# Attention and dense layers: four products with v in one go, maxima and closes in steps, five banks in one ring

## What is computed

```python
xn = _layernorm(x)
x = x + _L0_attn_ref(xn, ...) + _L0_ffn_ref(xn, ...)
xn = _layernorm(x)
x = x + _L1_attn_ref(xn, ...) + _L1_ffn_ref(xn, ...)
```

## Time and profile before

| | |
|---|---|
| median of three runs | 2231.34 us (2224.88 to 2234.45) |
| the profiled execution, its own time | 2234.62 us |
| its span, first to last instruction | 2232.8 us |
| mean granted TensorE clock | 0.924 |
| TensorE, matmuls | 1884.2 us busy (84%) |
| VectorE | 1211.5 us (54%) |
| ScalarE | 1096.7 us (49%) |
| GpSimd | 824.9 us (37%) |
| TensorE's part of the chain that ended last | 63% |

### The profile page before, as it was taken

One profiled execution on the slowest core, in us unless ns is written; L12 is line 12 of the kernel. 1 busy time (PEld: TensorE's weight loads), 2 busy tenths in 40 slices (PEclk: granted clock), 3 DMA queues, 4 the chain that ended last, 5 costly groups with the idle time before them and its releaser, 6 DMA issues.

```text
span 2232.8 us, 32221 instructions
## 1 busy us (share of the span) xinstructions
PE 1884.2 (84%) x10777; PEld 910.8 (41%) x10777; DVE 1211.5 (54%) x3653; ACT 1096.7 (49%) x2178; POOL 824.9 (37%) x935
## 2 busy tenths in 40 slices
PE   3573899999799999988778888888888898888877
PEld 2340455555245444422333444444344443444334
DVE  4554455555544444467555646657566565664653
ACT  0232455565455555545554545446455464554544
POOL 2215221111011111155575545465454554552520
PEclk8566899999999999989998999999999999999999
DMA  7244343333634244445234534344434344352240
GB/s 144 70 143 125 72 83 78 79 74 86 194 59 65 45 60 60 67 98 72 37 55 58 72 49 60 51 64 58 58 52 69 47 57 70 44 72 39 36 52 20
DMA packets 145972, 155.91 MB, mean 70 GB/s; under 512 B 26008, under 2 KB 132784, under 8 KB 145808
## 3 DMA queue, kind: packets, MB, share of 16 engines
q1 hardware_dynamic: 123872, 114.75, 33.1%
q0 software_dynamic: 10048, 14.44, 3.8%
q10 hardware_dynamic: 11888, 24.64, 3.2%
HBM read 55.95 MB, written 33.72 MB: 40 GB/s over the span
## 4 chain that ended last, share of the span: by engine, by line
PE 63%; DVE 10%; ACT 7%; POOL 7%; issue 6%; DMA 4%; SPq 3%; ACTq 0%; DVEq 0%; POOLq 0%
PE p_PV L937 11%; PE p_S L897 9%; PE p_S L918 8%; PE p_Mb L990 3%; PE p_S L1013 3%; DVE p_S L1125 3%; SPq L1884 3%; ACT t_R L1478 3%; PE p_Ma L870 2%; PE p_S L922 2%; PE p_S L870 2%; DMA t_NM<-hTd 2%; PE p_Mb L870 1%; PE p_Ma L806 1%; PE p_Mb L806 1%
## 5 line engine op out<-in xcount | busy, mean ns | idle before, releaser
L1478 ACT ACTIVATE t_R<-p_S 128x512 f32<-128x512 f32 (+1 forms) x1216 | 676.8, 575 | 489.3 <-PE p_S L922 269.8
L1125 DVE CUSTOM_DVE_ANT_0 p_S<-p_S,t_R 128x128 f32<-128x128 f32 (+3 forms) x1024 | 478.5, 515 | 295.0 <-PE p_S L897 294.7
L918 PE MATMUL p_S<-t_R 99*128 99x512 bf16 (+3 forms) x1536 | 485.5, 341 | 65.7 <-ACT t_R L1478 64.5
L897 PE MATMUL p_S<-t_R 96*128 96x512 bf16 (+3 forms) x1536 | 465.9, 344 | 83.2 <-DVE t_mx L1125 38.5
L1131 DVE TENSOR_REDUCE t_mx<-p_S 128x1 f32<-128x512 f32 x512 | 345.2, 684 | 303.4 <-PE p_S L897 277.7
L937 PE MATMUL p_PV<-t_R 128*17 128x512 f32 (+3 forms) x3072 | 338.6, 514 | 4.2 <-ACT t_R L1478 2.8
L897 PEld LDWEIGHTS p_S<-t_R 96*128 96x128 bf16 x1536 | 138.1, 99 | 414.5 <-issue 149.8
L918 PEld LDWEIGHTS p_S<-t_R 99*128 99x128 bf16 x1536 | 154.2, 100 | 218.5 <-ACT t_R L1478 112.9
L1681 POOL CAST t_spl<-t_rr 128x512 bf16<-128x512 f32 x80 | 49.0, 613 | 436.9 <-DVE t_rr L1088 436.9
L922 PE MATMUL p_S<-t_R,t_B1T 128*128 128x128 bf16 x1024 | 204.7, 225 | 0.0
L1125 DVE DVE_READ_ACCUMULATOR2_ANT t_mx<- 128x1 f32 x1024 | 142.4, 139 | 0.0
(11 more groups left out here) (299 smaller groups left out, 2505.7 us busy)
## 6 DMA issues: line engine op xcount, KB each, us to landing
t_R<-t_spl SPq DMA_DIRECT2D x480, 128.0 KB
t_R<-in_w ACTq DMA_DIRECT2D x32, 512.0 KB, 10.7
t_R<-ks SPq DMA_DIRECT2D x96, 128.0 KB
ks<-t_spl SPq DMA_DIRECT2D x16, 384.0 KB, 7.1
hTd<-t_NM SPq DMA_DIRECT2D x39, 128.0 KB
ysd<-t_NM SPq DMA_DIRECT2D x39, 128.0 KB
t_NM<-hTd SPq DMA_DIRECT2D x39, 128.0 KB, 2.3
ysd<-t_NM POOLq DMA_DIRECT2D x39, 128.0 KB, 3.1
```

Source lines behind the costliest of these rows:

```text
L897: t = self.nc.tensor.matmul(bank[:, z, :], qa[0:96, h, qb * 128:(qb + 1) * 128], ka[0:96, h, 0:n], start=True, stop=True)
L918: t = self.nc.tensor.matmul(bank[:, z, :], ka[0:99, h, kb * 128:(kb + 1) * 128], qa[0:99, h, n0:512], start=True, stop=not u.causal)
L1125: x = nc.vector.tensor_tensor_reduce(out=sc, in0=sc, in1=m.maskq[:, 512 - n:512], scale=1.0, scalar=NEG, op0=ALU.add, op1=ALU.max, accum_o ...
L1478: nc.scalar.activation(m.P1X[kb][j0 // per] if u.causal else m.P[p % 2][:, j0:j0 + per, :], m.s2_bank(k)[:, 0:per * n].rearrange("p (j n) ...
```

## The change

**Products.** In layer 1 `expp` keeps all four key blocks of a group, and `finish` issues their four products in one step, after the second scores of the next group. In layer 0 each key block stays by itself.

**Closes.** `finish` no longer adds steps. It sets a generator `closing`, of which each scores step without a `finish` takes one step: unload, in layer 1 an empty one, TensorE's `turn_o`, then `settle`.

**Maxima.** `maxp` becomes `top` (product and maximum) and a generator `shift`, of which each `top` but the first of a group takes one step during the next group: `turn_m` (TensorE), `shift_first` (ScalarE, the first of the four small instructions) and `shift_rest` (VectorE, the second), `shift_second` (ScalarE, the third), `shift_third` (VectorE, the fourth), `shift_rows` (SP).

**Projections.** A projection takes three steps: `project` on TensorE; `first` on ScalarE and `rest` on VectorE; `spread` on GpSimd and SP. v takes two, `project` and `keep`. The convolution does the same. The lane's empty tail grows from 9 (or 6) to 26 steps, the head start of the first and last convolution from 5 to 18.

**Banks.** `MB` gets the two banks of the maxima as fourth and fifth. Up to round 14 three go round, and `top` uses the other two in turn. From round 15 on five go round and the causal `top` takes from the same ring. The turned maxima take a bank of the ring in both layers.

**Experts.** The two halves of `up` and of `down` are one step each; the shares per round are rescaled (40 to 28, 24 to 14, 35 to 21).

```diff
@@ rounds
+        if i == 15:
+            e.ring = 5
         if 1 <= i < 6:
-            lanes.append(take(first, 40))
+            lanes.append(take(first, 28))
@@ Memory
-        self.MB = [ps("Ma"), ps("Mb"), self.S1[2]]
+        self.MB = [ps("Ma"), ps("Mb"), self.S1[2], self.S1[0], self.S1[1]]
@@ Engine.bank
         self.banks += 1
-        return self.banks % 3
+        return self.banks % self.ring
+
+    def top_bank(self, u):
+
+        if u.causal:
+            return self.bank()
+        self.tops += 1
+        return 3 + self.tops % 2
@@ Engine.pre
                 if u.b in (0, NB - 1):
-                    yield from steps(5)
+                    yield from steps(18)
                 for cc in range(2):
                     self.turn_c(u.b, cc, self.bank())
                     yield
-            self.convolve(u, self.bank())
-            yield
-            yield from steps(6)
+            i = self.bank()
+            self.convolve(u, i)
+            yield
+            self.first(u, 0, i)
+            self.rest(u, 0, i)
+            yield
+            self.spread(u, 0)
+            self.spread(u, 1)
+            yield
+            yield from steps(26)
             return
@@ Engine.project_unit
-        for z in range(3):
-            self.project0(u, z, self.bank())
-            yield
+
+        for z in range(2):
+            i = self.bank()
+            self.project(u, z, i)
+            yield
+            self.first(u, z, i)
+            self.rest(u, z, i)
+            yield
+            self.spread(u, z)
+            yield
+        i = self.bank()
+        self.project(u, 2, i)
+        yield
+        self.keep(u, i)
+        yield
@@ Engine.maxp
     def maxp(self, u):
-        return steps(s1_uses(u))
+
+        for g in range(2):
+            for x, p in enumerate(packs_of(u)):
+                self.top(u, g, p, self.top_bank(u))
+                if x:
+                    next(self.chain, None)
+                yield
+            self.chain = self.shift(u, g)
+        if u.n == 47:
+            yield from self.chain
+    def shift(self, u, g):
+
+        i = self.bank()
+        self.turn_m(u, g, i)
+        yield
+        self.shift_first(u, g, i)
+        self.shift_rest(u, g, i)
+        yield
+        self.shift_second(u, g)
+        yield
+        self.shift_third(u, g)
+        yield
+        self.shift_rows(u, g)
+        yield
@@ Engine.expp
                     self.scores(u, g, kb, j0, per, n0)
                     if self.late is not None and j0 + per >= 2:
-                        yield from self.finish()
+                        self.finish()
+                    else:
+                        next(self.closing, None)
                     yield
-                self.late = (u, g, kb)
+                if not u.causal:
+                    self.late = (u, g, (kb,))
+            if u.causal:
+                self.late = (u, g, range(4))
         if u.n == 47:
-            yield from self.finish()
+            self.finish()
+            yield from self.closing
 
     def finish(self):
 
-        (u, g, kb), self.late = self.late, None
-        self.product(u, g, kb)
-        if kb == 3:
-            yield
-            self.unload(u, g)
-            yield
-            self.settle(u, g, self.bank() if u.kind else None)
-            yield
+        (u, g, kbs), self.late = self.late, None
+        for kb in kbs:
+            self.product(u, g, kb)
+        if kbs[-1] == 3:
+            self.closing = self.close(u, g)
+
+    def close(self, u, g):
+
+        self.unload(u, g)
+        yield
+        if u.kind:
+            yield
+            i = self.bank()
+            self.turn_o(u, g, i)
+            yield
+            self.settle(u, g, i)
+        else:
+            self.settle(u, g, None)
+        yield
@@ TensorE
+    def turn_m(self, u, g, i):
+        e, m, s = self.e, self.m, self.s
+        M = self.mbank(i, s.mt_res, 2 * u.n + g + 1)
+        e.wait_ge(s.s1_read, tops_to(u, g))
+        self.nc.tensor.transpose(M[0:16, 0:128], m.mx[:, g, :], m.ident[:, :]).then_inc(s.mt_mm, 1)
@@ ScalarE
+    def shift_first(self, u, g, i):
+        e, m, s, n = self.e, self.m, self.s, 2 * u.n + g + 1
+        e.wait_ge(s.mt_mm, n)
+        if g:
+            e.wait_ge(s.d_mq[u.buf][0], 48 * u.fill)
+        elif u.n:
+            e.wait_ge(s.d_mq[(u.n - 1) % 3][1], 48 * ((u.n - 1) // 3 + 1))
+        self.nc.scalar.activation(m.msp[:, 0, :], m.MB[i][0:16, 0:128], ACT.Copy, scale=-1.0).then_inc(s.mt_first, 1)
+
+    def shift_second(self, u, g):
+        e, m, s, n = self.e, self.m, self.s, 2 * u.n + g + 1
+        e.wait_ge(s.mt_res, n)
+        self.nc.scalar.copy(m.msp[:, 1, :], m.mrr[:, :]).then_inc(s.mt_second, 1)
```

More of the change, by code:

```diff
@@ L106, in exps_before, with none @@
     return before + sum(exps_of(u, k % 4) for k in range(4 * g + kb))
+def none():
+    return iter(())
 def steps(n):
@@ L175, in rounds @@
         if i == 7:
-            lanes.append(chain(steps(12), take(second, 24)))
+            lanes.append(chain(steps(12), take(second, 14)))
         if 8 <= i < 13:
-            lanes.append(take(second, 35 if i < 12 else 60))
+            lanes.append(take(second, 21 if i < 12 else 60))
         if i == 13:
@@ L452, in __init__ @@
         self.late = None
-        self.banks = 0
+        self.chain = self.closing = none()
+        self.ring, self.banks, self.tops = 3, 0, 0
         if engine is not None:
@@ L683, in forward @@
     def forward(self, b):
-        self.inner(b, self.bank())
+        i = self.bank()
+        self.inner(b, i)
+        self.inner_first(b, i)
+        self.inner_rest(b, i)
         yield
@@ new lines, in top @@
+        (qb, js), n = p, 128 * (p[0] + 1) if u.causal else 512
+        self.s1 += 1
+        i = 4 * js[0] + qb
+        e.wait_ge(s.s1_mm, self.s1)
+        if u.causal:
+            e.wait_ge(s.masks, 4)
+            for z in range(len(js)):
+                sc = m.MB[b][:, z * n:z * n + n]
+                x = nc.vector.tensor_tensor_reduce(
+                    out=sc, in0=sc, in1=m.maskq[:, 512 - n:512], scale=1.0, scalar=NEG, op0=ALU.add, op1=ALU.max,
+                    accum_out=m.mx[:, g, i + 4 * z:i + 4 * z + 1])
+        else:
+            x = nc.vector.tensor_reduce(m.mx[:, g, i:i + 1], m.MB[b][:, :], AX.X, ALU.max)
```

180 lines of the change are left out of this document (70 added, 110 removed).

## The result

The changed kernel takes 2390.19 us (median of four runs, 2386.39 to 2397.80) against 2231.56 us before: a ratio of 1.072, with an interval of 1.068 to 1.076. The forecast was 2080. The profiled execution has a span of 2396.0 us against 2232.8.

A forecast was written before the change was run, and what follows sets the result against it. TensorE leads in both layers; layer 1's holes come from order, not load. Gains 31 + 38 + 39 + 26 + 28 + 5 + 25 = 192, losses 32 + 5 = 37, net 155: 2234.6 - 155 = 2080 us, range 2045 to 2120.

The forecast's parts named there:

- The slower one: Rival: after each burst exponentials run behind and TensorE starves at the scores, 30 us slower, 2265 us; chance 0.07.
- the burst: Layer 1 group ends: ScalarE stands still while the first exponential waits for the joined products; 32 us lost (0 to 96).
- products joined: Layer 1's four products with v per group in one go save 0.16 us per join, 192 joins: 31 us (0 to 44).
- turn of the maxima in steps: Turn moved behind the next group's second product, so TensorE stops waiting for the last maximum (L903): 38 us gained.
- turn of O in steps: Turn moved two scores behind ScalarE's unload, so TensorE's waits at L950 go: 39 us gained.
- five banks: One ring lets TensorE run up to four products ahead of VectorE, cutting L897's waits: 26 us gained (0 to 51).
- projections in steps: GpSimd's split no longer queues behind an unfinished convolution: 28 us in layer 1; hT waits in layer 0: 5 us.
- clock: With long holes gone, half of layer 1's loss from running at 1.2 GHz comes back: 25 us (0 to 48).
- The waits for hT in layer 0: TensorE waits 10.7 us at L990; SP reaching its wait later was to gain 5 us (0 to 15).

The follow-up runs named there:

- rows in their own round: Changed kernel, but each unit's second group closes its maxima and issues their rows at the end of its own round: 2211.55 us, ratio 0.990.
- single again: Changed kernel with the maxima's rows back in their own round, and layer 1's products issued one by one again: 2230.18 us, ratio 1.002.
- joined on before: Kernel before the change with only the four products of a layer 1 group in one go: 2228.47 us, ratio 0.998.
- one step: Maxima: 2126 us kernel (ScalarE's copy apart), both groups' maxima closed in one step, 2100.46 us. Projections: rows-in-own-round kernel, projections and convolution in one step, 2153.12 us.
- three empty steps: Kernel of 2100 us (both groups' maxima closed in one step) plus three empty steps behind a unit's last step: 2194.71 us, ratio 0.982.
- closes as before: 2126 us kernel (rows in own round, projections in one step, ScalarE's copy apart) with a group's close as before the change: 2180.30 us, ratio 0.979.
- ring of three: Changed kernel with rows in their own round, layer 1 back to three ring banks and two for the maxima: 2226.09 us, ratio 0.999.
- the last kernel: 2126 us kernel (ScalarE's copy apart) with maxima closed in steps for a unit's first group, in one step for its second: 2096.10 us, ratio 0.938.

## Why the prediction was wrong

**The step that failed** is that the move of the maxima's rows on SyncE's queue stands in the sum at nothing. One sentence of the prediction deals with that queue: "The SP DMAs of a projection (six of q or k) are issued in the same later step; the next unit needs them a round later, so they cost nothing there." It asked who waits for the moved DMAs, and not who stands behind them, and it dealt with the projections alone. The rows of a unit's second group moved as well, from the end of a round into the next, in layer 1 to the sixth of its lane's 22 steps, about a quarter of the round. There they stand behind the twelve DMAs. The moved rows are needed by the middle of that round, what the twelve DMAs bring only at its end. The price is 184 us, more than the whole forecast gain. 134 us appear when the rows alone are moved in the kernel before, where TensorE waits 111.7 us for them and not 209.5; why the changed kernel pays more was not tested. The later step of the projections' own DMAs was not the cause: with the projections in one step and the rows late the waits are 203.7 us.

None of the rivals was this. The slower one (2265 us) had TensorE starved by ScalarE behind the burst, and the trace does show ScalarE standing 397.8 us for the products; but the kernel that differs in the rows' place alone has the same burst, with 184.0 us of such standing, and is 1% faster than before. The mechanism that I called "for it" by the earlier trace rows, one waiting instruction at the head of a queue, was the right one, at another queue.

The other terms:

| term | forecast, us | measured, us | by |
|---|---|---|---|
| rows of the maxima past the DMAs | none | -184 | rows in their own round |
| products joined, less the burst | 31 - 32 | +28 (on before: +4) | single again; joined on before |
| turn of the maxima in steps | 38 | -19 with its tail, +68 at equal lane length | one step; three empty steps |
| turn of O in steps | 39 | +62 | closes as before |
| five banks | 26 | +21 | ring of three |
| projections in steps | 28 + 5 | -49 | one step |
| clock | 25 | in the rows above | granted clock 0.88 to 1.00 |

*Joined products.* The block is there as forecast, 32 instructions of 2.35 us drawn:

```profile
1387.52 2.35 PE L1035 MATMUL p_PV<-t_R 128*17 128x512 f32 x32
...
1389.80 0.39 PE L994 MATMUL p_S<-t_R 96*128 96x256 bf16 x2
```

From its start to the next product it is 2.28 us. Four single ones, an estimate by the prediction's slope, take 0.98 + 0.77 + 0.56 + 0.35 to the next start and 0.09 ahead of each, 3.02 in all; the block has its 0.09 once, 2.37. So a join is worth 0.65 / 3 = 0.22 us and 192 joins 42 us; I had taken 0.16 from the only joined pair. With 28 measured net, the burst cost some 14 us and not 32. The prediction had weighed a rule of the Trainium skill, TensorEngine Tiling (Array Packing), Key Properties, that only a change of the tiling mode drains TensorE, not a change of the tile within one. By that rule the whole 0.23 us goes, and the 0.22 measured here agree. Why the join brings nothing that can be told on the kernel before was not tested; its waits for exponentials grew by 46 us there.

*Turns.* Both waits went, as the rows of waits show. The size of the turn of O was low by a third. With the closes as before the turn waits 33.5 us for the unload, against 6.2, but the waits for exponentials also grow, from 73.6 to 106.1 us, and the sum had nothing for these. The clock of the whole execution is 0.93 in both kernels, so it isn't that. The turn of the maxima was read as free, "behind the second product of the next group"; that is so for a unit's first group. For the second it needs either the next round, which is the crossing of the DMAs, or a tail of steps, which costs more than the spacing brings. This part of the weave, that adding a step to a lane moves every other step of it, is in the prediction only for the convolution.

*The ring* came nearly as forecast.

*Projections in steps.* The 28 us were to come from GpSimd's split no longer queueing behind the convolution's cast. It still does, as the changed kernel's trace shows around the same wait as the earlier trace rows:

```profile
1510.39 0.69 DVE L1290 TENSOR_TENSOR t_R<-p_Mb,t_R 128x512 f32<-128x512 f32 x1 [6.72 <-ACT t_R L1599]
...
1512.89 0.61 POOL L1763 CAST t_spl<-t_rr 128x512 bf16<-128x512 f32 x1 [18.72 <-DVE t_rr L1184]
...
1518.29 1.15 POOL L1821 TENSOR_TENSOR t_R<-t_R 128x512 bf16<-128x512 f32 x1
...
1519.53 0.62 ACT L1606 COPY t_R<-t_R 64x512 bf16<-64x512 bf16 x1 [5.52 <-POOL t_R L1821]
...
1520.72 0.39 PE L1016 MATMUL p_S<-t_R 99*128 99x256 bf16 x1 [6.09 <-ACT t_R L1565]
```

The wait is 6.09 us here, 4.56 before. I had argued by places in the lanes that the split comes after the cast in issue order, and took the cast to be done by then; it is not, since it also waits for TensorE's convolution and VectorE's residue. The gain was real but needed another edit: 36 us with ScalarE's copy in a step of its own. The waits for hT in layer 0 went as forecast (15.4 us over both banks before, 2.5 after), though no run times that alone. What I did not look for at all was the load of x in front of the first projection, 47 us in layer 0 with what came with it.

*Clock.* The prediction had half of the slow time coming back. Where the holes went it came back whole (1.00 over 800 us of layer 1 in the last kernel); where they grew it fell to 0.88. What that is worth in time is less than the stretches at the lower level are long: 6.9 of the 29.9 us a period that the rows' place costs.

**Right**, then, were the readings of which waits stood in layer 1 and that they can go: the best kernel has 2096 us, 16 from the forecast of 2080. It has all parts of the change but three, the second group's maxima in steps, the rows late and the projections in steps, and one edit that the change does not have. That the two numbers are near each other is largely chance, as the table's terms show. These were measured on different kernels and need not add up; they do so roughly, to 141 us of the 160 lost.

**Open:** how much of the 68 us of spacing is ScalarE's share of the small steps and how much their distance was not measured. Nor was why three empty steps cost 88 us, by closeness or by the places of the other steps, and whether ScalarE's 173 us of issuing are the 92 us that remain with the rows on its queue.

## What to carry to other kernels

When work is moved in an order fixed beforehand, list for each instruction that goes with it, DMAs first, what it will now stand behind on its queue, and compare the due times: a small transfer that is waited for next must not be queued behind large ones that are due only later. When steps are spaced out, count what the extra steps do to the rest of their lane, a load and its first reader coming closer together, or three empty steps that cost 88 us. And if a change has several parts, time each alone: here parts worth +28, +62 and +21 us were hidden behind one of -184.

## What the runs showed of the hardware that I had not expected

Issuing is a cost of its own: twelve DMAs take SyncE's queue 4.91 + 3.81 = 8.7 us, 0.7 us each, and three rows of 4 KB each take 1.9 us. The cost is the same order on ScalarE's queue, 1.80 us for three, and there it holds up the exponentials. Behind the twelve DMAs the rows were usable 4.4 us after the last issue (1403.28 to 1407.71). Over the whole run the listing of DMAs gives a median of 5.3 us from issue to landing for rows in the changed kernel, and 1.7 in the kernel with the rows in their own round.

The same instructions of a period took from 126.2 to 167.4 us by their order and queue, with the busy times of VectorE, ScalarE and GpSimd within 3%. TensorE's went from 111.55 to 123.70 us, with a granted clock of 1.00 and of 0.88; the other 29 us are idle time. Short holes were enough for the clock to fall: five of 1.3 to 2.1 us in a period went with 0.94, and 0.50 right behind one of 2.01 us; a period with one hole of that length, 1.38 us, had 1.00.
